# A value sweep of a graph network: two of eight tiles scaled by ScalarE and added by TensorE instead of VectorE

## The chip, the cores and the metric

The kernel runs on one core of a Trainium2 chip. The metric is the device time of one execution in microseconds. The engines are called by their names here: TensorE (PE in the profile, PEld for its weight loads), VectorE (DVE), ScalarE (ACT), GpSimd (POOL) and SyncE (SP, which issues DMA transfers). A q behind an engine's name is its sequencer.

## The reference, cut to what matters

The program is a stack of four graph layers on 3125 nodes and 50000 edges, sorted by their target. Layer 2 is a pair of attention layers; the second of them has two heads of 128 channels. Its last step is the one that the change touches:

```python
def transformer_conv(x, src, dst, Wq, bq, Wk, bk, Wv, bv, Ws, bs, H, C, concat):
    ...
    v = (x @ Wv + bv).reshape(n, H, C)
    ...
    out = jax.ops.segment_sum(p[:, :, None] * v[src], dst, num_segments=n)
    out = out / denom[:, :, None]
    out = out.reshape(n, H * C) if concat else out.mean(axis=1)
    return out + x @ Ws + bs
```

Here H = 2, C = 128 and concat is false: the two heads are averaged. For each edge the values of both heads are weighted by their softmax weights, added, and summed over the edges of each target node. All in float32.

## The kernel before, in words

**Tiles.** The sorted edges are laid out as 416 tiles of 128 edges (one per partition). Each tile belongs to one block of 128 target nodes; the block's number is data, and stands in a table. A loop over all tiles is called a sweep. It runs 13 times (G) over four groups of eight tiles (S4 = 4, HU = 8). A group is called a half in the code, and half m = 4i + h. So a sweep has 52 halves. The ring buffer has four slots, one for each h.

**The sweep L2F.** The softmax weights of both heads lie in `alpha` (already divided by the denominator and halved). SyncE loads 1 MB per half from DRAM into the ring slot (lines 676 to 680, `values_in`): eight tiles of 256 values per edge, head 0 first, head 1 behind. It does so once TensorE has counted `ring_free`. Four engines then work on a half:
- VectorE (`mix`, lines 1675 to 1687): copies the weights of the half into `relw` (L1680), waits for the loaded rows, scales head 1 of all eight tiles in one operation (L1682), waits for TensorE's product of the half before the last and makes the one-hot matrices of edge and target (L1684 by way of the helper on L1092), waits for ScalarE's eight scalings, and adds head 0 to head 1 (L1687).
- ScalarE (`scale_l2f`, lines 1926 to 1934): waits for the copied weights and for the rows, and scales head 0 of the eight tiles, one activation each, by a scalar per partition (L1934).
- TensorE (`sums_f`, lines 2394 to 2405): loads the eight block numbers into registers (helper on L461), waits for one-hots and addition, and multiplies one-hot by mixed values, one product per tile, into the PSUM columns of the tile's block (L2401). In the trace one such float32 product is two LDWEIGHTS and two MATMUL instructions. Behind the last product it waits until it is done and frees the ring slot (L2404, L2405).

The order is fixed by hand, through semaphores: each engine has its own program of 52 halves. `relw` and the one-hots have two buffers (s = h % 2). The key line of TensorE:

```python
for k in range(HU):
    last = M.matmul(psum_blocks[:, ds(blocks[k], 1), :], ohv[:, (h % 2) * HU + k, :],
                    ring256[:, h * HU + k, F:2 * F].unsqueeze(1), start=False, stop=False)
```

Ahead of the sweep stands the softmax of layer 2 (all engines wait for it), and behind it VectorE adds the sums of all blocks to the node values (L1691) and layer 3 begins.

Of the kernel before, what the change touches and what calls it, by code (L numbers as in the profile page):

```python
# [25 lines left out]
def gnn_stack(nc, a, out):  # L26
    f32, bf16, i32 = mybir.dt.float32, mybir.dt.bfloat16, mybir.dt.int32
    ALU, ACT, AX = mybir.AluOpType, mybir.ActivationFunctionType, mybir.AxisListType.X
    ds = bass.ds
    x_in, src_in, dst_in, w_in = a["x"], a["src"], a["dst"], a["edge_weight"]  # L30

    P, F = 128, 128
# [6 lines left out]
    HU = 8  # L39
# [5 lines left out]
    U = S4 * HU  # L45
# [19 lines left out]
    with ctx:  # L65
        def sb(name, shape, dt=f32):
            return ctx.enter_context(nc.sbuf_tensor(name, shape, dt))

        def sem(name):
            return ctx.enter_context(nc.semaphore(name))  # L70
# [27 lines left out]
        alpha = sb("alpha", [P, T, 4])  # L98
# [23 lines left out]
        def carve(at, shape, dt=f32):  # L122
            return view(work, at, shape, dt)
# [7 lines left out]
        ring256 = carve(0, [U, 256])  # L131
# [21 lines left out]
        ohv = carve(8192, [2 * HU, P])  # L153
# [7 lines left out]
        relw = sb("relw", [P, 2, HU, 5])  # L161
# [103 lines left out]
        psum_blocks = psf[:, 0:NP].rearrange("p (b f) -> p b f", f=P)  # L265
# [106 lines left out]
        def ph(name):  # L372
            if name not in made:
                made[name] = sem(name)
            return made[name]
# [25 lines left out]
        VALUES = [2 * SENT[g] * HU * 16 + CB * 16 for g in range(NS)]  # L401
        assert NS == CH
        HEADS = (4, 4, 2)

        def softmax_order(H):
            late = [step for h in range(H) for step in ([("merged", h)] + ([("inverse", h - 1)] if h else []))]
            return [("shifted", h) for h in range(H)] + late + [("inverse", H - 1)]

        def sm_step(n, what, h):
            return sum(len(softmax_order(H)) for H in HEADS[:n]) + softmax_order(HEADS[n]).index((what, h)) + 1  # L410

        def sm_made(n, what, h):
            return 2 * sum(HEADS[:n]) + (HEADS[n] if what == "safe" else 0) + h + 1

# [6 lines left out]
        def half_no(i, h):  # L421
            return i * S4 + h
# [27 lines left out]
        def values_reloaded(i, h):  # L450
            return values_copied(G - 1, h) + (i + 1) * 16
# [13 lines left out]
        def tiles_of(i, h):  # L465
            return ds(i * U + h * HU, HU)
# [433 lines left out]
        def _(dve):  # L900
            V = nc.vector
# [189 lines left out]
            def one_hots(out_t, o, i, h, iota=iota_f[:, :]):  # L1091
                return V.tensor_tensor(out_t, rec[o][:, tiles_of(i, h), 1:2].to_broadcast([P, HU, P]),  # L1092
                                       iota.unsqueeze(1).to_broadcast([P, HU, P]), ALU.is_equal)
# [35 lines left out]
            with dve.Fori(0, CH) as i:  # L1129
                s = Steps(dve, ph("node_dve"), i, NLN, DONE["n0"])  # L1130
# [544 lines left out]
            def mix(i, h):  # L1675

                s = h % 2
                m = half_no(i, h)
                v = ring256[:, h * HU:(h + 1) * HU, F:2 * F]
                V.tensor_copy(relw[:, s, :, 1:3], alpha[:, tiles_of(i, h), 0:2]).then_inc(ph("L2F_weights"), 1)  # L1680
                dve.wait_ge(s_rows[h], values_reloaded(i, h))
                V.tensor_tensor(v, v, alpha[:, tiles_of(i, h), 1:2].to_broadcast([P, HU, F]), ALU.mult).then_inc(ph("L2F_mixed"), 1)  # L1682
                dve.wait_ge(ph("L2F_product"), m + 1)
                one_hots(ohv[:, s * HU:(s + 1) * HU, :], 1, i, h).then_inc(ph("L2F_onehot"), 1)  # L1684
                dve.wait_ge(ph("L2F_mixed"), 2 * m + 1)
                dve.wait_ge(ph("L2F_scaled"), m * HU + HU)
                V.tensor_tensor(v, v, ring256[:, h * HU:(h + 1) * HU, 0:F], ALU.add).then_inc(ph("L2F_mixed"), 1)  # L1687

            each_half(dve, mix)
            dve.wait_ge(ph("closed"), CLOSED["L2F"])  # L1690
            link(V.tensor_tensor(x[:, :, :], x[:, :, :], psum_blocks, ALU.add))  # L1691
# [38 lines left out]
        def _(act):  # L1730
            A = nc.scalar
# [194 lines left out]
            def scale_l2f(i, h):  # L1926

                s = h % 2
                m = half_no(i, h)
                act.wait_ge(ph("L2F_weights"), m + 1)  # L1930
                act.wait_ge(s_rows[h], values_reloaded(i, h))
                for k in range(HU):
                    v = ring256[:, h * HU + k, 0:F]
                    A.activation(v, v, ACT.Copy, scale=relw[:, s, k, 1:2]).then_inc(ph("L2F_scaled"), 1)  # L1934

            each_half(act, scale_l2f)

            root("n3")
# [13 lines left out]
        def _(pe):  # L1952
            M = nc.tensor
# [107 lines left out]
            with pe.Fori(0, CH) as i:  # L2061
                pe.wait_ge(ph("node_dve"), DONE["n0"] + i * NLN + NLN)
                for b in range(CB):
                    last = M.transpose(psf[:, b * P:(b + 1) * P], hs[:, b, :], ident[:, :])
# [3 lines left out]
                for b in range(CB):  # L2068
                    last = M.matmul(psf[:, 1024 + b * P:1024 + (b + 1) * P], hT[:, b * P:(b + 1) * P], w01[:, :],
                                    start=True, stop=True)  # L2070
# [56 lines left out]
            for bank in BANKS:  # L2127
                pe.wait_ge(ph("node_normed"), NORMED["n1"] + bank[-1] + 1)
                for b in bank:
                    last = M.transpose(psum_blocks[:, b, :], h_all[:, b, :], ident[:, :])  # L2130
                last.then_inc(ph("node_turned"), 1)
            for n, bank in enumerate(BANKS):
                pe.wait_ge(ph("node_hT"), HT["n1"] + n + 1)
                for b in bank:
                    nodes = hT_all[:, b * P:(b + 1) * P]
                    M.matmul(ps[:, 7, b * 8:(b + 1) * 8], nodes, watt[:, :], start=True, stop=True)
                    last = M.matmul(psum_blocks[:, b, :], nodes, wlin[:, :], start=True, stop=True)
# [91 lines left out]
            def blocks_of(o, i, h):  # L2229
                return loaded_blocks(mybir.EngineType.PE, o, i, h)  # L2230
# [95 lines left out]
            def by_heads(n, to, weights, last_head=0):  # L2326
                for h in range(4):
                    if last_head and h > 1:
                        pe.wait_ge(ph("n2b_h1"), last_head + h - 3)
                    last = M.matmul(to, acc[:, n, h * P:(h + 1) * P], weights(h), start=h == 0, stop=h == 3)  # L2330
                return last
# [22 lines left out]
            for n in range(NB):  # L2354
                if n >= 2:
                    pe.wait_ge(ph("n2b_evac"), NB + 2 + max(n - 3, -1))
                last = by_heads(n, ps[:, 4 + n % 4, 0:256], lambda h: wq2[h // 2][:, h % 2, :])
                if n < OVERWRITTEN:
                    last = by_heads(n, ps[:, 4 + n % 4, 256:384], lambda h: ws2[:, h, :])
# [35 lines left out]
            def sums_f(i, h):  # L2395
                m = half_no(i, h)
                blocks = blocks_of(1, i, h)
                pe.wait_ge(ph("L2F_onehot"), m + 1)
                pe.wait_ge(ph("L2F_mixed"), 2 * m + 2)
                for k in range(HU):  # L2400
                    last = M.matmul(psum_blocks[:, ds(blocks[k], 1), :], ohv[:, (h % 2) * HU + k, :],  # L2401
                                    ring256[:, h * HU + k, F:2 * F].unsqueeze(1), start=False, stop=False)
                last.then_inc(ph("L2F_product"), 1)
                pe.wait_ge(ph("L2F_product"), m + 3)  # L2404
                pe.sem_inc(ph("ring_free"), 1)  # L2405

            each_half(pe, sums_f)
            close_sums(7, zero_f).then_inc(ph("closed"), 1)

# [54 lines left out]
```

## Time and profile before

| | us |
|---|---|
| median of three runs | 5294.79 |
| lowest and highest | 5293.7, 5297.85 |
| span of the profiled execution, first to last instruction | 5289.8 |
| TensorE, VectorE, ScalarE, GpSimd busy in the span | 2873.2, 2794.9, 791.8, 3461.7 |
| sweep L2F, first weight copy to last product | 4482.15 to 4691.09 |

The profile is of one execution. No time of its own is given for it apart from its span; the median of the runs is 5.0 us above that span, which holds what lies ahead of the first and behind the last instruction. Busy time of TensorE counts overlapping matmuls once, and "idle before" is the time in which the engine ran nothing just ahead of the instruction. The name behind it is inferred: it is whoever last fulfilled a semaphore that the instruction waited for, even if that was long before. "Issue" means that nothing such was found. Granted clock 1.0 is 2.4 GHz, 0.5 is 1.2 GHz.

### The profile page before, as it was taken

The page shows a single profiled execution, that of the slowest core. Times are in us where ns is not written, and L with a number is a line of the kernel's source. Part 1 is how long each engine was busy: PE and PEld are TensorE (multiplying, and loading weights), DVE is VectorE, ACT ScalarE, POOL GpSimd, SP SyncE. Part 2 cuts the span into 40 slices and gives each one's busy share as a digit, 9 for nine tenths or more (in the row PEclk, how much of TensorE's full clock was granted, in tenths as well). Part 3 has the DMA queues.
Part 4 walks back from the last instruction along what each step waited for, and adds up shares of the span by engine and source line. Part 5 has one row for each costly group of instructions (what it writes and reads, how often), then busy time and mean ns, then how long its engine had stood idle before and what let it go on. Part 6 is the DMA issues. An engine that isn't in the chain of part 4 may idle for free.

```text
span 5289.8 us, 73813 instructions
## 1 busy us (share of the span) xinstructions
PE 2873.2 (54%) x17389; PEld 2236.2 (42%) x17390; DVE 2794.9 (53%) x6391; ACT 791.8 (15%) x3180; POOL 3461.7 (65%) x3922
## 2 busy tenths in 40 slices
PE   5443477763333573034445877768986665643333
PEld 5333366653333463034443333356464333543333
DVE  8889822223221588033335988876147666971111
ACT  2121100000000100000001555456100001640000
POOL 3777677767777777777774777654047773017775
PEclk9999955555555555556556999878997766876566
DMA  2211222231112483033333444534169997732223
GB/s 62 67 29 47 68 52 52 52 46 26 27 27 25 60 115 47 18 69 79 81 81 59 137 127 127 133 91 139 40 191 316 335 331 221 268 124 52 52 52 53
DMA packets 303759, 526.16 MB, mean 99 GB/s; under 512 B 89450, under 2 KB 172640, under 8 KB 296928
## 3 DMA queue, kind: packets, MB, share of 16 engines
q1 hardware_dynamic: 177960, 289.53, 19.3%
q0 software_dynamic: 125728, 235.82, 18.3%
q8 instruction: 27, 0.44, 0.0%
q14 instruction: 44, 0.36, 0.0%
HBM read 423.29 MB, written 101.80 MB: 99 GB/s over the span
## 4 chain that ended last, share of the span: by engine, by line
POOL 42%; issue 28%; DVE 14%; PE 9%; DMA 2%; ACT 2%; DVEq 2%; POOLq 1%; SPq 1%; ACTq 0%; PEldq 0%
POOL work L789 31%; POOL rec_by_dst L749 6%; PE ps L2330 3%; POOL acc L789 2%; DVE acc L1568 2%; ACT work L1934 1%; DVE work L1027 1%; PE ps L2104 1%; POOL idx_slot L783 1%; PE ps L2045 1%; DVE work L1015 1%; PE ps L2401 1%; DVE work L973 1%; DVE work L1042 1%; DVE acc L1496 1%
## 5 line engine op out<-in xcount | busy, mean ns | idle before, releaser
L789 POOL DMA_INDIRECT work<-t_h,idx_slot x832 | 801.2, 963 | 546.2 <-DMA t_h<-acc 304.5
L2045 PE MATMUL ps<-work 128*128 128x128 f32 (+1 forms) x2496 | 700.0, 443 | 677.2 <-DMA work<-t_v,idx_slot 352.0
L789 POOL DMA_INDIRECT work<-t_v,idx_slot x832 | 789.2, 949 | 267.0 <-issue 221.9
L2045 PEld LDWEIGHTS ps<-work 128*128 128x128 f32 x2496 | 583.2, 328 | 700.5 <-issue 700.5
L789 POOL DMA_INDIRECT work<-t_xl,idx_slot x416 | 413.5, 994 | 123.8 <-issue 111.0
L2298 PE MATMUL ps<-big,work 128*128 x832 | 411.3, 647 | 105.7 <-DVE work L1246 68.9
L749 POOL DMA_INDIRECT rec_by_dst<-sc_rec_d,sc_idx x392 | 394.1, 1005 | 113.2 <-issue 104.6
L749 POOL DMA_INDIRECT rec_by_src<-sc_rec_s,sc_idx x392 | 388.6, 991 | 113.3 <-issue 104.2
L2370 PE MATMUL ps<-big,work 128*128 x832 | 326.4, 549 | 191.7 <-DVE aS L1630 153.5
L1102 DVE COPY relw<-rec_s 128x16 f32 x104 | 19.7, 189 | 672.8 <-PE ps L2045 672.2
L789 POOL DMA_INDIRECT work<-t_kv,idx_slot x208 | 201.3, 968 | 257.7 <-DMA t_kv<-big 173.1
L2370 PEld LDWEIGHTS ps<-big,work 128*128 128x128 f32 x832 | 206.0, 268 | 311.6 <-issue 280.1
L2250 PE MATMUL ps<-work 128*128 128x128 f32 x832 | 196.0, 430 | 206.4 <-DVE work L1445 206.4
L1496 DVE TENSOR_TENSOR acc<-ps,work 128x512 f32<-128x512 f32 x416 | 278.9, 681 | 49.6 <-PE ps L2298 26.8
L2298 PEld LDWEIGHTS ps<-big,work 128*128 128x128 f32 x832 | 161.7, 204 | 317.1 <-issue 317.1
L2044 PEld LDWEIGHTS ps<-one_column,work 128*128 128x128 f32 x832 | 222.9, 327 | 167.7 <-issue 167.7
L1876 ACT ACTIVATE acc<-acc 128x128 f32<-128x128 f32 x832 | 250.0, 301 | 247.7 <-DVE acc L1496 247.2
L1092 DVE TENSOR_TENSOR work<-rec_d,ps 128x1024 f32<-128x1024 f32 x52 | 63.1, 1220 | 409.3 <-PE ps L2045 408.7
L1105 DVE TENSOR_SCALAR work<-ps,relw 128x128 f32<-128x128 f32 x832 | 274.5, 401 | 3.8
L2250 PEld LDWEIGHTS ps<-work 128*128 128x128 f32 x832 | 181.4, 330 | 211.0 <-issue 211.0
L2044 PE MATMUL ps<-one_column,work 128*128 128x1 f32 x832 | 183.7, 290 | 152.4 <-DMA work<-t_v,idx_slot 145.6
L789 POOL DMA_INDIRECT acc<-t_kv,idx_slot x208 | 202.7, 975 | 66.1 <-issue 54.9
(480 smaller groups left out, 6177.0 us busy)
## 6 DMA issues: line engine op xcount, KB each, us to landing
work<-rows_of_v_by_position SPq DMA_DIRECT2D x52, 1024.0 KB
work<-relT_by_dst SPq DMA_DIRECT2D x156, 256.0 KB
rows_of_h_by_position<-work SPq DMA_DIRECT2D x52, 512.0 KB
work<-rows_of_h_by_position SPq DMA_DIRECT2D x52, 512.0 KB
rows_of_v_by_position<-work SPq DMA_DIRECT2D x26, 1024.0 KB
rows_of_v_by_position<-acc SPq DMA_DIRECT2D x26, 1024.0 KB
work<-t_v,idx_slot POOLq DMA_INDIRECT x832
work<-relT_by_src SPq DMA_DIRECT2D x52, 256.0 KB
```

Of the source, the lines that this page charges most:

```text
L749: nc.gpsimd.indirect_dma_start(rec_dram[o], bass.IndirectOffsetOnAxis(ap=sc_idx[:, h * HU + k:h * HU + k + 1], axis=0), sc_rec[o][:, h * H ...
L789: nc.gpsimd.indirect_dma_start(to, None, table, bass.IndirectOffsetOnAxis(ap=idx_slot[:, h * HU + k:h * HU + k + 1], axis=0)).then_inc(s_g ...
L1105: last = V.tensor_scalar(oh[:, h * HU + k, :], iota_p, pair[:, k, 0:1], pair[:, k, 1:2], ALU.is_equal, ALU.mult)
L1496: V.tensor_tensor(prod[:, k, :].rearrange("p (h c) -> p h c", h=4), q, g, ALU.mult).then_inc(sig("L2A", "_multiplied"), 1)
L1568: V.tensor_tensor(part, part, ps[:, k, 0:4 * WN].rearrange("p (h j) -> p h j", j=WN), ALU.add).then_inc(ph("L2C_added"), 1)
L1876: ins = A.activation(q, q, ACT.Copy, accum_out=aS[:, s * HU + k, hd:hd + 1])
L2044: M.matmul(weights_sum[:, ds(b, 1)], oh[:, s, :], one_column[:, :], start=False, stop=False)
L2045: ins = M.matmul(psum_blocks[:, ds(b, 1), 0:width], oh[:, s, :], ring[:, h * HU + k, 0:width].unsqueeze(1), start=False, stop=False)
L2250: last = M.matmul(psum_blocks[:, ds(blocks[k], 1), :], oh[:, (h % 2) * HU + k, :], ring140[:, h * HU + k, 0:F].unsqueeze(1), start=False, ...
L2298: M.matmul(q_bank(h, k).unsqueeze(1), ohT[:, s, k * P:(k + 1) * P], big[:, ds(blocks[k], 1), :], start=True, stop=True).then_inc(sig("L2A" ...
L2330: last = M.matmul(to, acc[:, n, h * P:(h + 1) * P], weights(h), start=h == 0, stop=h == 3)
L2370: last = M.matmul(ps[:, k % 4, 0:256].unsqueeze(1), ohT[:, s, k * P:(k + 1) * P], q2[:, ds(blocks[k], 1), :], start=True, stop=True)
```

## The change

Of each half's eight tiles, six (MIXED) are treated as before. For the other two, VectorE neither scales nor adds; ScalarE scales both heads (SCALED = 2 x 8 - 6 = 10 activations per half instead of 8), and TensorE sums each head with a product of its own, with the same one-hot matrix, into the same PSUM columns. TensorE waits for all ten scalings ahead of the seventh tile. VectorE waits for the first six scalings of a half only. Its wait for TensorE's product of the half before the last moves from ahead of the one-hots to ahead of the weight copy.

```diff
--- before.py
+++ after.py
@@ -401,6 +401,8 @@
         VALUES = [2 * SENT[g] * HU * 16 + CB * 16 for g in range(NS)]
         assert NS == CH
         HEADS = (4, 4, 2)
+        MIXED = HU - 2
+        SCALED = 2 * HU - MIXED
 
         def softmax_order(H):
             late = [step for h in range(H) for step in ([("merged", h)] + ([("inverse", h - 1)] if h else []))]
@@ -1676,15 +1678,15 @@
 
                 s = h % 2
                 m = half_no(i, h)
-                v = ring256[:, h * HU:(h + 1) * HU, F:2 * F]
+                v = ring256[:, h * HU:h * HU + MIXED, F:2 * F]
+                dve.wait_ge(ph("L2F_product"), m + 1)
                 V.tensor_copy(relw[:, s, :, 1:3], alpha[:, tiles_of(i, h), 0:2]).then_inc(ph("L2F_weights"), 1)
                 dve.wait_ge(s_rows[h], values_reloaded(i, h))
-                V.tensor_tensor(v, v, alpha[:, tiles_of(i, h), 1:2].to_broadcast([P, HU, F]), ALU.mult).then_inc(ph("L2F_mixed"), 1)
-                dve.wait_ge(ph("L2F_product"), m + 1)
+                V.tensor_tensor(v, v, alpha[:, ds(i * U + h * HU, MIXED), 1:2].to_broadcast([P, MIXED, F]), ALU.mult).then_inc(ph("L2F_mixed"), 1)
                 one_hots(ohv[:, s * HU:(s + 1) * HU, :], 1, i, h).then_inc(ph("L2F_onehot"), 1)
                 dve.wait_ge(ph("L2F_mixed"), 2 * m + 1)
-                dve.wait_ge(ph("L2F_scaled"), m * HU + HU)
-                V.tensor_tensor(v, v, ring256[:, h * HU:(h + 1) * HU, 0:F], ALU.add).then_inc(ph("L2F_mixed"), 1)
+                dve.wait_ge(ph("L2F_scaled"), m * SCALED + MIXED)
+                V.tensor_tensor(v, v, ring256[:, h * HU:h * HU + MIXED, 0:F], ALU.add).then_inc(ph("L2F_mixed"), 1)
 
             each_half(dve, mix)
             dve.wait_ge(ph("closed"), CLOSED["L2F"])
@@ -1930,8 +1932,9 @@
                 act.wait_ge(ph("L2F_weights"), m + 1)
                 act.wait_ge(s_rows[h], values_reloaded(i, h))
                 for k in range(HU):
-                    v = ring256[:, h * HU + k, 0:F]
-                    A.activation(v, v, ACT.Copy, scale=relw[:, s, k, 1:2]).then_inc(ph("L2F_scaled"), 1)
+                    for head in range(1 if k < MIXED else 2):
+                        v = ring256[:, h * HU + k, head * F:(head + 1) * F]
+                        A.activation(v, v, ACT.Copy, scale=relw[:, s, k, 1 + head:2 + head]).then_inc(ph("L2F_scaled"), 1)
 
             each_half(act, scale_l2f)
 
@@ -2398,8 +2401,11 @@
                 pe.wait_ge(ph("L2F_onehot"), m + 1)
                 pe.wait_ge(ph("L2F_mixed"), 2 * m + 2)
                 for k in range(HU):
-                    last = M.matmul(psum_blocks[:, ds(blocks[k], 1), :], ohv[:, (h % 2) * HU + k, :],
-                                    ring256[:, h * HU + k, F:2 * F].unsqueeze(1), start=False, stop=False)
+                    if k == MIXED:
+                        pe.wait_ge(ph("L2F_scaled"), (m + 1) * SCALED)
+                    for head in ((1,) if k < MIXED else (0, 1)):
+                        last = M.matmul(psum_blocks[:, ds(blocks[k], 1), :], ohv[:, (h % 2) * HU + k, :],
+                                        ring256[:, h * HU + k, head * F:(head + 1) * F].unsqueeze(1), start=False, stop=False)
                 last.then_inc(ph("L2F_product"), 1)
                 pe.wait_ge(ph("L2F_product"), m + 3)
                 pe.sem_inc(ph("ring_free"), 1)
```

## Rows read from the trace of the kernel before

**Rows 1.** The page: its first line, and the chain of work by engine.

```profile
span 5289.8 us, 73813 instructions
...
POOL 42%; issue 28%; DVE 14%; PE 9%; DMA 2%; ACT 2%; DVEq 2%; POOLq 1%; SPq 1%; ACTq 0%; PEldq 0%
```

**Rows 2.** Windows: stretch, length; busy PE, PEld, DVE, ACT, POOL; granted clock, DMA share, GB/s.

```profile
4486.00:4691.00 205.00, 125.82 (x832) 115.27 (x832) 182.55 (x205) 126.02 (x409) 0.00 (x0) 0.86 0.72 246
...
3060.00:3140.00 80.00, 65.30 (x195) 27.87 (x194) 71.78 (x163) 44.13 (x259) 62.22 (x71) 0.94 0.44 130
...
3520.00:3670.00 150.00, 129.80 (x726) 107.31 (x725) 105.27 (x368) 117.19 (x467) 87.92 (x46) 0.99 0.53 154
```

**Rows 3.** Groups by line, 4482 to 4692 us: busy us, mean ns, idle before, releasers.

```profile
L1934 ACT ACTIVATE work<-work,relw 128x128 f32<-128x128 f32 x416 | 127.2, 388 | 75.3 <-DVE relw L1680 75.3
...
L2401 PE MATMUL ps<-work 128*128 128x128 f32 x832 | 125.9, 314 | 80.3 <-DVE work L1682 34.2 <-DVE work L1092 25.8 <-issue 15.6
...
L1687 DVE TENSOR_TENSOR work<-work 128x1024 f32<-128x1024 f32 x52 | 63.6, 1224 | 13.2 <-ACT work L1934 13.1
...
L1092 DVE TENSOR_TENSOR work<-rec_d,iota_f 128x1024 f32<-128x1024 f32 x52 | 63.4, 1218 | 5.1 <-PE ps L2401 5.1
...
L1682 DVE TENSOR_TENSOR work<-work,alpha 128x1024 f32<-128x1024 f32 x52 | 63.3, 1218 | 0.1
```

**Rows 4.** Timeline of VectorE and ScalarE (start us, us): first addition, then one round.

```profile
4484.93 1.23 DVE L1687 TENSOR_TENSOR work<-work 128x1024 f32<-128x1024 f32 x1 [0.19 <-ACT work L1934]
...
4560.46 1.22 DVE L1682 TENSOR_TENSOR work<-work,alpha 128x1024 f32<-128x1024 f32 x1
...
4563.16 1.22 DVE L1687 TENSOR_TENSOR work<-work 128x1024 f32<-128x1024 f32 x1 [0.34 <-ACT work L1934]
...
4564.30 0.17 DVE L1680 COPY relw<-alpha 128x16 f32 x1
...
4564.50 2.44 ACT L1934 ACTIVATE work<-work,relw 128x128 f32<-128x128 f32 x8 [1.38 <-DVE relw L1680]
```

**Rows 5.** Timeline of TensorE's halves in the sweep: start us, us, instructions, idle before.

```profile
4486.31 3.78 PE L2401 MATMUL ps<-work 128*128 128x128 f32 x16 [1.45 <-DVE work L1687]
...
4491.66 2.05 PE L2401 MATMUL ps<-work 128*128 128x128 f32 x16 [1.58 <-DVE work L1682]
...
4546.16 2.05 PE L2401 MATMUL ps<-work 128*128 128x128 f32 x16 [1.39 <-DVE work L1682]
...
4550.11 2.58 PE L2401 MATMUL ps<-work 128*128 128x128 f32 x16 [1.91 <-DVE work L1682]
...
4554.17 3.78 PE L2401 MATMUL ps<-work 128*128 128x128 f32 x16 [1.48 <-DVE work L1682]
...
4559.34 2.05 PE L2401 MATMUL ps<-work 128*128 128x128 f32 x16 [1.39 <-DVE work L1092]
...
4562.80 2.05 PE L2401 MATMUL ps<-work 128*128 128x128 f32 x16 [1.41 <-issue]
...
4689.04 2.05 PE L2401 MATMUL ps<-work 128*128 128x128 f32 x16 [1.41 <-issue]
```

**Rows 6.** Line 461 in the sweep, TensorE's sequencer: durations in ns, min/median/max.

```profile
L461 PEldq TENSOR_LOAD <-block_of_tile_d x104: 327/331/334, 4482.2 to 4688.4; - x104
...
L461 PEldq FUSED_REGOPS  x91: 46/46/46, 4482.6 to 4688.3; - x91
```

**Rows 7.** Waits of SyncE's queue in the sweep (us, times, longest), and one load, issue to landing.

```profile
SPq L678 <- PEq L2405: 189.2, 48, 41.0
...
4627.12 4.65 DMA work<-rows_of_v_by_position
```

**Rows 8.** Groups by line and shape: a 640-wide VectorE operation elsewhere.

```profile
L1702 DVE TENSOR_TENSOR acc<-acc,rows 128x640 f32<-128x640 f32 x5 | 4.1, 824 | 0.2
```

**Rows 9.** Timelines cut short: seven instructions at full clock, six at low clock.

```profile
4562.80 1.04 PE L2401 MATMUL ps<-work 128*128 128x128 f32 x7 [1.41 <-issue]
...
4554.17 1.64 PE L2401 MATMUL ps<-work 128*128 128x128 f32 x6 [1.48 <-DVE work L1682]
```


## The prediction

> **What bounds the kernel now.** I read the page first, for the span and the chain [rows 1]. The chain names GpSimd for 42% of the whole kernel, which says nothing about the stretch that the diff touches. So I looked for that stretch: the value sweep of layer 2 runs from the first weight copy at 4482.15 us to the last product at 4691.09 us, 4% of the span. GpSimd does nothing in it [rows 2].
>
> Inside it the share of busy time points at VectorE: 182.55 of 205 us, 89%, against 61% for TensorE and 61% for ScalarE [rows 2]. Per half of eight tiles VectorE runs a copy, the scaling of head 1, the one-hots and the addition, each large one about 1.22 us [rows 3], and comes round every 3.8 to 3.9 us: in [rows 4] the scaling of head 1 begins 3.84 us before the next copy. Before its addition it waits 0.34 us for ScalarE's eight scalings (2.44 us). ScalarE in turn waits for the weights, which VectorE copies only after the addition. That is a loop of two engines at 3.87 us.
>
> TensorE has to be read in another way, by its order in time [rows 5]. A half is 16 matmul instructions (two for each of eight products) and takes 2.05 us at 2.4 GHz or 3.78 us at 1.2 GHz. Between two halves stand 1.4 to 1.5 us, or 1.9 us once in four halves, where the loop turns (one early gap has 1.58). These gaps name a VectorE line or "issue" as what ended them, but their length does not change with it: 1.39 us stands with either of two VectorE lines, 1.41 us with "issue". In the gap the sequencer waits for its own last product, frees the ring slot and loads the next eight block numbers (two loads of 0.331 us [rows 6] and register work). So the named releaser had long been done, and the gap is TensorE's own. The account closes: 52 halves are busy for 125.9 us, the gaps are 80.3 us less the 1.45 us ahead of the first, and 125.9 + 78.9 = 204.8 us [rows 3]; from first to last product the trace has 4689.04 + 2.05 - 4486.31 = 204.8 us [rows 5]. **TensorE is never kept waiting in the sweep**. At its mean clock it needs 3.94 us per half, slightly more than VectorE's 3.87, and VectorE is sometimes held back by it: 5.1 us ahead of the one-hots [rows 3]. Of the 125.9 us, 52 x 2.05 = 106.6 would be left at full clock; 19.3 us are the price of the low clock (mean 0.86 in [rows 2]).
>
> The transfers are not the limit: SyncE spends 189.2 us waiting for TensorE's free slots, and a load lands 4.65 us after issue [rows 7], while its slot is wanted three halves later.
>
> **The change part by part.**
> - VectorE: scaling and addition shrink from 1024 to 768 elements. A 640-wide one takes 0.824 us [rows 8] and a 1024-wide one 1.22, so 768 takes about 0.96: 0.53 us less per half. Cover: none of it is on TensorE's path, so I count it at nothing. VectorE would go to about 3.3 us per half, then wait for TensorE.
> - ScalarE: ten scalings instead of eight, 2.44 / 8 x 2 = 0.61 us more, 3.05 us per half. VectorE waits for the first six only (1.83 us). TensorE waits for all ten, in the middle of its half. This is hidden as long as ScalarE needs less than TensorE's period of 4.0 us.
> - TensorE: two products more per half, four instructions. Their spacing at full clock is (2.05 - 1.04) / (16 - 7) = 0.112 us and at low clock (3.78 - 1.64) / (16 - 6) = 0.214 us [rows 5, 9]. At full clock 52 x 4 x 0.112 = **+23.3 us**. The gaps stay.
> - The new wait of TensorE before tile six has no row like it. Lower bound nothing, because the sequencer runs ahead of the array; a gain is excluded, since nothing is taken away. Upper bound: a stop of one semaphore step, about 0.05 us as in [rows 6]'s register work, 2.6 us in all. I take nothing, since [rows 5] show 16 instructions without a break although each tile has its own address step. Behind it are queued only the two last tiles' products, and then the freeing of the slot.
> - The moved wait: VectorE now waits for the product of two halves before ahead of the weights, not ahead of the one-hots. Queued behind it are copy, scaling, one-hots and addition, and ScalarE waits for the copy. From that product on, about 0.1 + 0.96 + 1.22 + 0.96 = 3.2 us pass to the end of the addition (3.3 us to the end of ScalarE's tenth). TensorE needs the half only after gap, half and gap, 1.4 + 2.5 + 1.4 = 5.3 us. Cost nothing, with 2 us of cover. No DMA queue is passed: SyncE waits only for freed slots, and they come later, so the loads have more time.
> - The low clock. Lower bound: nothing, all halves at 2.4 GHz. Upper bound: the same share as now, 19.3 x 129.9 / 106.6 = 24 us. Each fall follows a long gap and shows in two halves, as in [rows 5], (2.58 - 2.05) + 1.73 = 2.3 us; the sweep has eight such pairs besides the low first half. A low half would now be busy 4.6 of 6.1 us, 75%, near the dense stretches with 82% and 87% busy, where the granted clock is 0.94 and 0.99 [rows 2]; a half at full clock is busy 2.5 of 4.0, 62%, near the sweep as it is. So I expect it to fall as often but to come back in half the time: 12 us, **7 us less** than the 19.3 of now.
> - The start: the first addition waits 0.19 us [rows 4]; with that and two shorter steps (0.27 each) TensorE begins 0.7 us earlier. **-0.7 us**. The end is TensorE's last product, as before.
>
> Sum: 23.3 - 7.3 - 0.7 = +15.3 us on a span of 5289.8, that is 5305.1. The median of the three runs, 5294.79, stands 5.0 us above that span (start and end of the execution), so the forecast is **5310 us**.
>
> The Trainium skill, Perfetto Trace Analysis, section Identifying the Most-Contended Engine, says to find the engine with the highest occupancy and to optimize that one first. By it VectorE with 89% would be the bound and the change a gain; the order in time disagrees.
>
> **Rivals.**
> - VectorE is the bound (the other side). Place: the additions at the end of VectorE's round. Price: 52 x 0.53 = 27.6 us gained, 5267 us. For it: 89% busy, and 60.0 of TensorE's 80.3 idle us name a VectorE line [rows 3]. Against it: the constant gaps. It decides from the point where TensorE's half plus gap is shorter than VectorE's round; with twenty instructions it is 2.50 + 1.55 = 4.05 us at best, above today's 3.87. Chance 0.05.
> - The clock stays up: twenty instructions per half keep TensorE at 2.4 GHz throughout. 52 x 2.50 + 78.9 = 208.8 us of sweep, +3.3 with the earlier start, 5298 us. For it: 0.99 in the densest stretch. Against it: the long gap of 1.91 us, ahead of each fall, is still there. Chance 0.10. The Trainium skill, TensorE: Matmul & The Clock Gate, Part 1, states that the gate is closed by default and activity opens it; more activity would then mean the full clock. The trace agrees in direction only: the denser stretches have the higher clock.
> - The moved wait closes a circle: product, weights, ten scalings, product. If its 3.3 us were 2.5 us longer than I think (a scaling slowed by transfers, say), TensorE would wait 0.5 us per half: 26 us more, 5336 us. Against it: ScalarE's groups last 2.44 or 2.45 us under the same transfers. Chance 0.04.
> - The change doesn't do what it says: the output or the order is the same as before and the time 5295. The counts in the diff (ten scalings, six awaited) fit each other. Chance 0.01.
> - My forecast, TensorE bound with a partly lower clock: 0.80.
>
> **How the numbers follow.** The forecast alone has a low-clock term between 0 and 24 us, 5298 to 5322, and with the bound of the mid-half wait and a few us between runs up to 5326. That with the full-clock case is the range, 5298 to 5326. About 0.2% (10.6 us) is what a measurement of this kernel can tell from no change. The full-clock case and the lower part of the forecast (a low-clock term under 7 us) lie within it, 0.10 + 0.08, and the case of no change 0.01: 0.19. Faster is the first rival, 0.05. The rest is slower, 0.76.
>
> **What would show it.** Right: L2401 with 1040 matmuls, busy for 140 to 145 us, the gaps unchanged at 1.4 and 1.9 us, the sweep at 221 us from first to last product; VectorE's waits move to the product (about 0.7 us per half, ahead of the weights); ScalarE's groups of 3.05 us. Wrong: gaps of TensorE that grow and vary, a wait on L1934 ahead of a product, or a sweep under 205 us. The clock term is wrong if the granted clock in the sweep stays at 0.86 or reaches 1.

## The result, and the profile after

The changed kernel takes 5310.26 us (median of six runs, 5308.27 to 5318.01) against 5294.24 us of the kernel before (six runs): ratio 1.0032, 95% interval 1.0022 to 1.0042. That is **16 us slower**. The forecast was 5310 us. The profiled execution took 5315.45 us with a span of 5313.0. The stretch of interest, from first to last product of the sweep, has 4710.76 + 2.49 - 4491.66 = 221.6 us; before it had 204.8. These 16.8 us account for the whole difference of the medians, 16.0 us. The span grew by 23.2 us: 5.35 us of it lie ahead of the changed lines (the first product comes that much later than before), and 1.0 us behind the sweep. In experiments 1 to 4 the first product came between 4484.64 and 4489.16 us, so this start scatters by some us.

First the window of the sweep after, columns as in [rows 2]:

```profile
4491.00:4713.00 222.00, 142.19 (x1040) 133.08 (x1040) 159.93 (x205) 156.54 (x514) 0.00 (x0) 0.93 0.66 227
```

VectorE went from 182.55 to 159.93 us of busy time, and the time rose all the same. TensorE went from 125.82 to 142.19 us, and its granted clock from 0.86 to 0.93. The same stretch by line, to be held against [rows 3]:

```profile
L1937 ACT ACTIVATE work<-work,relw 128x128 f32<-128x128 f32 x520 | 157.7, 388 | 63.3 <-DVE relw L1683 63.3
L2407 PE MATMUL ps<-work 128*128 128x128 f32 x1040 | 142.5, 298 | 79.9 <-DVE work L1685 77.8 <-issue 1.4 <-DVE work L1689 0.7
...
L1094 DVE TENSOR_TENSOR work<-rec_d,iota_f 128x1024 f32<-128x1024 f32 x52 | 63.3, 1218 | 0.0
L1685 DVE TENSOR_TENSOR work<-work,alpha 128x768 f32<-128x768 f32 x52 | 49.8, 958 | 1.7
L1689 DVE TENSOR_TENSOR work<-work 128x768 f32<-128x768 f32 x52 | 49.4, 951 | 0.0
L1683 DVE COPY relw<-alpha 128x16 f32 x52 | 9.2, 177 | 59.2 <-PE ps L2407 56.1 <-PEq L2395 3.0
```

TensorE's account again: 142.5 us busy and 79.9 us idle, of which 0.75 stand ahead of the first half; 142.5 + 79.15 = 221.6. The idle time is what it was before (78.9 us between halves). What is new is 56.1 us that VectorE waits for TensorE's product ahead of the weight copy (L1683), and ScalarE's waits behind it. TensorE in order of time, the answer to [rows 5]:

```profile
4491.66 4.61 PE L2407 MATMUL ps<-work 128*128 128x128 f32 x20 [0.75 <-DVE work L1689]
4497.74 2.49 PE L2407 MATMUL ps<-work 128*128 128x128 f32 x20 [1.48 <-DVE work L1685]
4501.65 2.49 PE L2407 MATMUL ps<-work 128*128 128x128 f32 x20 [1.42 <-DVE work L1685]
...
4521.68 2.49 PE L2407 MATMUL ps<-work 128*128 128x128 f32 x20 [1.38 <-DVE work L1685]
4526.08 3.96 PE L2407 MATMUL ps<-work 128*128 128x128 f32 x20 [1.91 <-DVE work L1685]
4531.52 2.49 PE L2407 MATMUL ps<-work 128*128 128x128 f32 x20 [1.47 <-DVE work L1685]
4535.42 2.49 PE L2407 MATMUL ps<-work 128*128 128x128 f32 x20 [1.42 <-DVE work L1685]
...
4710.76 2.49 PE L2407 MATMUL ps<-work 128*128 128x128 f32 x20 [1.39 <-issue]
```

And VectorE's first weight copy, from its timeline:

```profile
4488.30 0.18 DVE L1683 COPY relw<-alpha 128x16 f32 x1 [3.02 <-PEq L2395]
```

TensorE's gaps are 1.38 to 1.48 us, and 1.90 to 2.08 at the turn of the loop (before: 1.91 to 1.97), though VectorE now finishes each half longer ahead. The plainest sign is the time from the end of the addition that a half needs to the start of that half. One pair from the kernel before (its addition is the one at 4563.16 in [rows 4], which ends at 4564.38), then one from the changed kernel:

```profile
4566.78 1.97 PE L2401 MATMUL ps<-work 128*128 128x128 f32 x16 [1.94 <-DVE work L1092]
...
4566.46 0.95 DVE L1689 TENSOR_TENSOR work<-work 128x768 f32<-128x768 f32 x1
4569.44 2.49 PE L2407 MATMUL ps<-work 128*128 128x128 f32 x20 [1.42 <-DVE work L1685]
```

That is 2.40 us of slack before and 2.03 us after. Over all halves but the first the slack is 0.81 to 3.80 us before and 2.01 to 4.30 us after. Only the first half of the sweep starts 0.15 us behind its addition, and so waits for it. (The addition is the last thing that a half needs from VectorE; the one-hots end before it.) Nearly all gaps of the changed kernel name the same line, L1685, the scaling of head 1, which is not what TensorE waits for; the name tells nothing here, and the slack does. A half is 2.49 us at full clock. The low clock shows in one half at a time (3.96 us at 4526.08), where in [rows 5] it showed in two.

### The profile page after: what moved, and what is told of

It is laid out like the page before. It is cut to its first block, busy times and chain, and to the rows that moved or that the text cites. A ratio compares the mean times of both kernels' runs of the same rounds, so it can differ in the third digit from the quotient of the medians.

```text
span 5313.0 us, 74385 instructions
## 1 busy us (share of the span) xinstructions
PE 2885.2 (54%) x17597; PEld 2250.0 (42%) x17598; DVE 2769.1 (52%) x6391; ACT 822.3 (15%) x3284; POOL 3462.3 (65%) x3922
## 3 DMA queue, kind: packets, MB, share of 16 engines
q1 hardware_dynamic: 177960, 289.53, 19.4%
## 4 chain that ended last, share of the span: by engine, by line
POOL 41%; issue 27%; DVE 15%; PE 11%; DMA 2%; DVEq 2%; POOLq 1%; SPq 1%; ACT 1%; ACTq 0%; PEldq 0%
POOL work L791 31%; POOL rec_by_dst L751 6%; PE ps L2333 3%; PE ps L2407 3%; POOL acc L791 2%; DVE acc L1570 2%; DVE work L1029 1%; PE ps L2107 1%; POOL idx_slot L785 1%; PE ps L2048 1%; DVE work L1685 1%; DVE work L1017 1%; DVE work L975 1%; DMA work<-t_v,idx_slot 1%; DVE work L1044 1%
```

## The experiments

Theory T: TensorE bounds the sweep, with its products and a gap of its own sequencer. Its rivals: VectorE's round bounds it (V), or the moved wait closes a circle (C). All experiments change only the sweep. The sweep is measured from first to last product in the profiled execution. The total time is the median beside the kernel before of the same group.

**1. VectorE's relief alone.** The kernel before, `mix` over six tiles:

```diff
-v = ring256[:, h * HU:(h + 1) * HU, F:2 * F]
+v = ring256[:, h * HU:h * HU + 6, F:2 * F]
...
-V.tensor_tensor(v, v, ring256[:, h * HU:(h + 1) * HU, 0:F], ALU.add)...
+V.tensor_tensor(v, v, ring256[:, h * HU:h * HU + 6, 0:F], ALU.add)...
```

The weights in the scaling of head 1 are cut to the same six tiles.

> The kernel before, with VectorE scaling and adding only six of the eight tiles of each half; ScalarE (eight scalings) and TensorE (sixteen instructions) are untouched. Left out: head 0 and the weight of head 1 in two of eight tiles. If TensorE bounds the sweep: from first to last product 204 to 205 us as before, gaps of 1.4 and 1.9 us as before, the time within 3 us of the kernel before; VectorE only waits longer for the product. If VectorE's round bounds it: 52 x 0.53 = 28 us less, a sweep of 177 us, 5267 us.

Measured: 5294.18 us against 5295.1, ratio 0.9999 (0.9989 to 1.0009); sweep 203.0 us. The groups by line of its sweep:

```profile
L2401 PE MATMUL ps<-work 128*128 128x128 f32 x832 | 124.2, 311 | 80.0 <-DVE work L1092 65.0 <-DVE work L1682 12.4 <-issue 1.4
...
L1092 DVE TENSOR_TENSOR work<-rec_d,iota_f 128x1024 f32<-128x1024 f32 x52 | 63.7, 1224 | 32.0 <-PE ps L2401 31.8
L1687 DVE TENSOR_TENSOR work<-work 128x768 f32<-128x768 f32 x52 | 49.7, 956 | 9.7 <-ACT work L1934 8.9
```

Some 27 us of VectorE's work left and nothing came of it: its waiting for TensorE ahead of the one-hots grew from 5.1 to 31.8 us. V falls. (The sweep is 1.8 us shorter than before. TensorE is busy for 1.7 us less at the same number of instructions, and a half at full clock is 2.05 us in both: the low clock took 17.6 us here and 19.3 there.)

**2. The added products taken out of the changed kernel.**

```diff
-for head in ((1,) if k < MIXED else (0, 1)):
+for head in (1,):
```

> The changed kernel without the two extra products of a half: VectorE and ScalarE as changed, TensorE with sixteen instructions again, its wait for ten scalings kept. Left out: head 0 of two of eight tiles. If TensorE's four instructions are the whole cost: sweep back at about 204 us (52 x 2.05 + 78.9 + a low-clock term near 19), total near 5294. If the moved wait or the two more scalings cost anything: it stays over 5300 and the gaps of TensorE grow and vary.

Measured: 5295.5 us, ratio 1.0003 (0.9994 to 1.0013); sweep 206.1 us.

```profile
L1937 ACT ACTIVATE work<-work,relw 128x128 f32<-128x128 f32 x520 | 157.6, 388 | 48.8 <-DVE relw L1683 48.7
L2407 PE MATMUL ps<-work 128*128 128x128 f32 x832 | 127.0, 316 | 79.9 <-DVE work L1685 77.7 <-issue 1.4 <-DVE work L1689 0.7
...
L1683 DVE COPY relw<-alpha 128x16 f32 x52 | 9.2, 178 | 44.5 <-PE ps L2407 41.5 <-PEq L2395 3.0
```

The moved wait, the ten scalings and TensorE's wait amid the half are all still there, and the loss is gone. So these three cost nothing that the time or the gaps show. The sweep is 1.3 us longer than before, again by TensorE's low clock (20.4 us of it).

**3. The added products alone, in the kernel before.**

```diff
 for k in range(HU):
-    last = M.matmul(..., ring256[:, h * HU + k, F:2 * F].unsqueeze(1), ...)
+    for head in ((1,) if k < 6 else (0, 1)):
+        last = M.matmul(..., ring256[:, h * HU + k, head * F:(head + 1) * F].unsqueeze(1), ...)
```

> The kernel before, with a second product (head 0 region) for two of eight tiles and nothing else changed: VectorE and ScalarE do all of their old work. Changed in the result: head 0 of those two tiles is counted twice. If TensorE bounds the sweep: 52 x 2.49 + 78.9 + 12 = 220 us or so, total 5310, the same as the changed kernel, because VectorE's round of 3.87 us stays under 4.05. If VectorE's round bounds it: no more than 3 us above the kernel before.

Measured: 5308.23 us, ratio 1.0028 (1.0017 to 1.0038); sweep 220.6 us.

```profile
L2402 PE MATMUL ps<-work 128*128 128x128 f32 x1040 | 141.8, 297 | 80.3 <-DVE work L1092 77.4 <-DVE work L1687 1.4 <-issue 1.4
...
L1092 DVE TENSOR_TENSOR work<-rec_d,iota_f 128x1024 f32<-128x1024 f32 x52 | 63.7, 1225 | 31.8 <-PE ps L2402 31.5
```

Four instructions more per half reproduce the loss, with all of VectorE's work in place. TensorE's busy time, 141.8 us, is that of the changed kernel within 1 us. With 2 and 3 the cause is shown from both sides.

**4. The wait put back.** The changed kernel, with VectorE's wait ahead of the one-hots again:

```diff
-dve.wait_ge(ph("L2F_product"), m + 1)
 V.tensor_copy(relw[:, s, :, 1:3], alpha[:, tiles_of(i, h), 0:2])...
 ...
+dve.wait_ge(ph("L2F_product"), m + 1)
 one_hots(ohv[:, s * HU:(s + 1) * HU, :], 1, i, h)...
```

> The changed kernel with VectorE's wait for the product put back to where it was, ahead of the one-hots. If the moved wait is covered by TensorE's own work (my account: 2 us of cover): same sweep of 221 us, same 5310. If it closes a circle of product, weights and scalings: several us less than the changed kernel, with TensorE's gaps shorter.

Measured: 5311.14 us, ratio 1.0032 (1.0021 to 1.0044), the changed kernel's own; sweep 221.1 us.

```profile
L2407 PE MATMUL ps<-work 128*128 128x128 f32 x1040 | 142.1, 297 | 79.7 <-DVE work L1094 72.2 <-issue 6.9 <-DVE work L1689 0.6
...
L1094 DVE TENSOR_TENSOR work<-rec_d,iota_f 128x1024 f32<-128x1024 f32 x52 | 63.7, 1225 | 60.8 <-PE ps L2407 60.8
```

VectorE's wait moved back to the one-hots and has about the same size (60.8 us). C falls for the changed kernel: where VectorE waits for TensorE makes no difference while it has to wait anyway.

**5 to 8. TensorE's own gap.** If the gap is the loading of the next block numbers and not a wait, then loading them while the products run must shorten it. The products are all issued by then; the sequencer does the loads ahead of its wait for their end. In the first half behind the turn of the loop they stay where they were:

```diff
-def sums_f(i, h):
+def sums_f(i, h, blocks):
     m = half_no(i, h)
-    blocks = blocks_of(1, i, h)
     ...
     last.then_inc(ph("L2F_product"), 1)
+    nxt = blocks_of(1, i, h + 1) if h < S4 - 1 else None
     pe.wait_ge(ph("L2F_product"), m + 3)
     pe.sem_inc(ph("ring_free"), 1)
+    return nxt
...
-each_half(pe, sums_f)
+with pe.Fori(0, G) as i:
+    blocks = blocks_of(1, i, 0)
+    for h in range(S4):
+        blocks = sums_f(i, h, blocks)
```

This group of four, and the two groups behind it, ran on other chips, on which the kernel before took 6702 to 6760 us. The 1400 us more lie outside the sweep, nearly all ahead of it: in the first trace of this group the first product of the sweep comes at 5850.30 us instead of 4486.31, and the first sort loop (L1971) alone ends at 818 us instead of 413. The kernel before was not traced there, so its sweep is taken as the 204.8 us of the first chip; the changed kernel, traced on both, has 221.6 and 221.8 us. So in this part differences in microseconds say more than ratios. Totals scatter more than sweeps: in the four traces of this group the first product comes between 5813.71 and 5850.30 us, while what follows the last one lasts 663.7 to 665.5 us.

Early loading in the kernel before (5):

> The kernel before, with TensorE's block numbers of the next half loaded while the products of this half still run (for three of four halves; the first after the turn of the loop is as before). If the gap is TensorE's own sequencer work, three of four gaps shrink from 1.4 to 0.3 or 0.5 us where nothing else is late, and then the round of VectorE and ScalarE (3.87 us per half) bounds the sweep: about 201 us instead of 205, total 5288 to 5293, with waits of TensorE on VectorE's addition that vary. If the gap is a wait for VectorE or for the product, it stays and the time too.

Measured: 6693.99 against 6702.02 us, ratio 0.9988 (0.9966 to 1.001), by itself no change that can be told; sweep 199.3 us. Its timeline:

```profile
5901.03 2.05 PE L2400 MATMUL ps<-work 128*128 128x128 f32 x16 [0.49 <-PE ps L2400]
...
5903.10 1.22 DVE L1687 TENSOR_TENSOR work<-work 128x1024 f32<-128x1024 f32 x1 [0.33 <-ACT work L1934]
...
5904.46 2.05 PE L2400 MATMUL ps<-work 128*128 128x128 f32 x16 [1.39 <-DVE work L1687]
...
5906.93 1.23 DVE L1687 TENSOR_TENSOR work<-work 128x1024 f32<-128x1024 f32 x1 [0.26 <-ACT work L1934]
...
5908.29 1.86 PEld L2400 LDWEIGHTS ps<-work 128*128 128x128 f32 x16 [1.97 <-issue]
...
5910.84 1.22 DVE L1687 TENSOR_TENSOR work<-work 128x1024 f32<-128x1024 f32 x1 [0.34 <-ACT work L1934]
```

Now the gap varies, from 0.40 to 1.86 us apart from the turn of the loop, and the releaser is mostly the addition (L1687). It is a real wait this time: an addition ends at 5903.10 + 1.22 = 5904.32 and the half begins at 5904.46, the next ends at 5908.16 and the half begins at 5908.29. A start 0.13 to 0.15 us behind its addition is what a real wait looks like in these traces. VectorE and ScalarE bound the sweep, at 3.8 to 3.9 us per half.

Early loading in the changed kernel (6):

> The changed kernel with the same early loading of block numbers. If TensorE's own gap is what turned the change into a loss: TensorE needs 2.49 + (1.9 + 3 x 0.35) / 4 = 3.23 us per half at full clock, VectorE and ScalarE need about 3.2, a 1 MB load about 3.4 to 3.5. The sweep falls from 221 to 175 to 190 us, the total to 5268 to 5282, below the kernel before. If the gap is a wait for others: no difference.

Measured: 6662.08 us, 39.9 under the kernel before, ratio 0.9946 (0.992 to 0.9973); sweep 177.6 us.

```profile
L2406 PE MATMUL ps<-work 128*128 128x128 f32 x1040 | 134.7, 287 | 43.7 <-DVE work L1685 23.6 <-DVE work L1689 13.8 <-PE ps L2406 6.3
...
L1683 DVE COPY relw<-alpha 128x16 f32 x52 | 9.0, 172 | 22.4 <-PE ps L2406 19.4 <-PEq L2395 3.0
```

```profile
5899.45 2.49 PE L2406 MATMUL ps<-work 128*128 128x128 f32 x20 [0.48 <-DVE work L1689]
5904.02 2.40 PE L2406 MATMUL ps<-work 128*128 128x128 f32 x20 [2.07 <-DVE work L1685]
5906.91 2.49 PE L2406 MATMUL ps<-work 128*128 128x128 f32 x20 [0.49 <-PE ps L2406]
5909.92 2.49 PE L2406 MATMUL ps<-work 128*128 128x128 f32 x20 [0.52 <-DVE work L1689]
5912.90 2.49 PE L2406 MATMUL ps<-work 128*128 128x128 f32 x20 [0.49 <-DVE work L1689]
```

The first of these two blocks has the groups by line, the second TensorE's halves. Three of four gaps are 0.48 to 0.52 us now, the one at the turn of the loop is as it was (1.90 to 2.08 us), and the idle time fell from 79.9 to 43.7 us. VectorE's waits for the product fell from 56.1 to 19.4 us. The total gained more than the expected 5268 to 5282 us would mean (13 to 27 us under a kernel before of 5295); the sweep gives 27 of the 39.9 us.

These gaps are as even as those of the changed kernel, and yet two of them in every four halves are waits:

```profile
5908.83 0.95 DVE L1689 TENSOR_TENSOR work<-work 128x768 f32<-128x768 f32 x1
5911.80 0.96 DVE L1689 TENSOR_TENSOR work<-work 128x768 f32<-128x768 f32 x1
```

The additions end at 5909.78 and 5912.76 us, and the halves start 0.14 us behind each, at 5909.92 and 5912.90. So it goes in the third and fourth half of every turn, while the first two have 1.47 us of slack or more (but for the very first half of the sweep). The waits are short, since TensorE's shortest gap with early loads is 0.40 us (in experiment 5), but TensorE and VectorE are now about even. In the third half even C's chain closes: the product that ends at 5906.42 releases the weight copy at 5906.58, and VectorE works without a break from there to 5909.78. What putting the moved wait back would give here was not run. The transfers are not the limit: SyncE still waits 164.1 us for free slots, and the DMA engines are busy for 0.80 of the time. The 3.4 to 3.5 us that this expectation and that of experiment 8 give for a load are shown by no run; 283 GB/s at that busy share would make it about 3 us, as an estimate.

More products per half, with the gap left as it is (7; MIXED = HU - 4, four tiles each way):

> The changed kernel with four of eight tiles mixed by VectorE and four added by TensorE (twelve scalings, 24 matmul instructions per half). TensorE bound: 52 x (2.49 + 0.45) + 78.9 + a low-clock term of about 13 = 245 us, total 5333, i.e. as much above the changed kernel as it is above the one before, and somewhat more. VectorE bound: below the changed kernel.

Measured: 6738.2 us, 36.2 above the kernel before, ratio 1.0048 (1.003 to 1.0066); sweep 242.1 us.

```profile
L2407 PE MATMUL ps<-work 128*128 128x128 f32 x1248 | 163.2, 291 | 79.1 <-DVE work L1685 71.3 <-issue 7.6 <-DVE work L1689 0.2
```

TensorE has 163.2 us of work and still 79.1 of gaps. From eight to six to four mixed tiles the sweep goes 204.8, 221.6, 242.1 us: 16.8 and 20.5 us more for 208 instructions more each time, while VectorE has less to do each time (the expectation of 245 us was 3 us too high).

Early loading with seven mixed tiles (8):

> Early loading of block numbers, with seven of eight tiles mixed by VectorE (nine scalings, 18 matmul instructions). Per half VectorE about 3.4 us, ScalarE 2.7, TensorE 2.27 + 0.74 = 3.0, a load 3.4 to 3.5. Within 5 us of the same kernel with six mixed tiles, and below both kernels: 5268 to 5285.

Measured: 6678.59 us, 23.4 under the kernel before, ratio 0.9963 (0.994 to 0.9985); sweep 181.2 us.

```profile
L2406 PE MATMUL ps<-work 128*128 128x128 f32 x936 | 122.4, 287 | 59.9 <-DVE work L1689 58.5 <-PE ps L2406 1.5
...
L1689 DVE TENSOR_TENSOR work<-work 128x896 f32<-128x896 f32 x52 | 56.8, 1092 | 5.5 <-ACT work L1937 2.3
```

TensorE's 59.9 us of gaps now name the addition for 58.5, and the starts bear it out:

```profile
5907.23 1.09 DVE L1689 TENSOR_TENSOR work<-work 128x896 f32<-128x896 f32 x1
5908.47 2.27 PE L2406 MATMUL ps<-work 128*128 128x128 f32 x18 [1.13 <-DVE work L1689]
```

This half starts 0.15 us behind the end of its addition (5908.32), with a gap of 1.13 us. With seven mixed tiles VectorE's round bounds the sweep again; it waits only 2.3 us for ScalarE and 3.0 us for TensorE in all. The two kernels are 3.6 us apart in the sweep, within the 5 expected; their totals are 16 us apart, more than the sweep explains, and both scatter by 30 us and more on this chip. Where the rest comes from stays open.

**The version that beats both, again.** Its expectations and those of its companions:

> The changed kernel with early loading of block numbers, a second time, since the group of runs before it ran with a kernel before of 6702 us, 1400 us of it outside this sweep. If the gain lies in the sweep alone, it is the same number of microseconds wherever the rest stands: a sweep of 178 us, 27 us less than the 205 of the kernel before, and a total 24 to 32 us under the kernel before beside it (5263 to 5270 where that is 5294).

> The kernel before with early loading of block numbers, a second time: a sweep of 199 to 201 us, bounded by the round of VectorE and ScalarE (52 x 3.87 = 201), 4 to 6 us under the kernel before beside it, with TensorE's gaps of changing length (0.5 to 2 us) and its starts at the ends of VectorE's additions.

> The changed kernel with early loading of block numbers, a third time, beside the changed kernel itself in the same group. A sweep of 178 us; 24 to 32 us under the kernel before and 40 to 48 us under the changed kernel, on whichever chip.

> The changed kernel as it is: a sweep of 221 to 222 us and 15 to 17 us above the kernel before of the same group, on whichever chip, because the difference is TensorE's work in the sweep.

| kernel | sweep, us | less the kernel before of its group, us | ratio and interval |
|---|---|---|---|
| changed, early loads, 2nd | 175.7 | -47.4 | 0.9936 (0.9912 to 0.9961) |
| before, early loads, 2nd | 201.1 | -25.9 | 0.9976 (0.9958 to 0.9995) |
| changed, early loads, 3rd | 177.6 | -27.8 | 0.9958 (0.9938 to 0.9978) |
| changed, again | 221.8 | +16.1 | 1.0018 (0.9995 to 1.0042) |

The interval of the changed kernel includes no change here; it also holds the 1.0032 of the first measurement. The sweeps repeat within 2 us on every chip. The total times scatter much more on these chips: in three groups the changed kernel with early loads is 39.9, 47.4 and 27.8 us under the kernel before, where its sweep is 27 to 29 us shorter than 204.8. For the last two 24 to 32 us were expected, and only the third measurement is there. The second run of the kernel before with early loads gained 25.9 us where its sweep gives 4 and 4 to 6 were expected. These misses have no cause in the sweep, and they stay open. Side by side on one chip, the changed kernel with early loads is 43.9 us under the changed kernel (6732.59 and 6776.46), and the sweeps differ by 44.2. On a chip of the first kind it was not run; by the sweep alone it would stand near 5294 - 27 = 5267 us there, as an estimate.

## Why the prediction was right

Point by point, by its own steps:

- **TensorE never waits in the sweep**: shown, but for the first half. Relieving VectorE alone changed nothing (1), the gaps kept their length in the changed kernel and in experiments 1 to 4 and 7, whose VectorE and ScalarE had different loads, and every half but the first starts 0.8 us or more behind its addition. One step of the argument proved nothing: "the account closes" holds for any engine, since busy and idle time always add up to the stretch.
- **Four instructions per half, +23.3 us at full clock**: a half has 2.49 us instead of 2.05, 52 x 0.44 = 22.9 us. The gaps added 0.25 us (79.15 instead of 78.9).
- **The low clock, 12 us where 19.3 were**: measured is 142.5 - 52 x 2.49 = 13.0. The granted clock of the sweep rose to 0.93. Two more kernels with twenty instructions and long gaps have 12.3 (3) and 12.6 us (4), so the size repeats. The reason I gave, as many falls and each half as dear, holds only roughly: behind the first half, seven halves lose 1.5 us each, where eight pairs lost 2.2. That is one fall fewer, each at two thirds of the price and not at half. The two misses cancel, and the number was the middle of a range of 24 us: that it met so well is partly luck.
- **Start, -0.7 us**: from the first weight copy to the first product it was 4486.31 - 4482.15 = 4.16 us and is now 4491.66 - 4488.30 = 3.36, that is 0.8 less.
- **The wait amid the half and the moved wait, nothing**: shown by 2, 3 and 4. Twenty instructions run through in 2.49 us, less than the 2.50 of sixteen plus four spacings.
- **VectorE and ScalarE**: operations of 958 and 951 ns for the forecast 0.96 us, groups of 3.03 us for 3.05. VectorE's wait was given as 0.7 us per half; it is 56.1 / 52 = 1.1. I had set its round of 3.3 us against TensorE's 4.05 at full clock; the true numbers are about 3.2 and 4.26.
- **The sum**: from the first weight copy to the last product +15.3 us were forecast, and 224.95 - 208.94 = 16.0 are measured; the medians differ by 16.0 too. From first to last product it is 16.0 forecast against 16.8.
- **The 5.0 us between span and median** are not "start and end of the execution", as the prediction and the section on the time before have it. In every run a time stands 1.7 to 3.0 us above its own span; the rest of the 5.0 is that the profiled execution was shorter than the median one. As an offset from one execution to the median it did no harm.

The rule of the Trainium skill, Perfetto Trace Analysis, section Identifying the Most-Contended Engine (highest occupancy first), would have picked VectorE with its 89%. For TensorE that section goes by the busy time of the weight loads, here 115.27 of 205 us or 56%, which is lower still. Runs 1 and 3 show that TensorE, with 61% in its matmuls, was the bound. Its other 39% were gaps in which no other engine held it up, and experiment 6 took almost half of that idle time away by moving the loads of the block numbers. The same page's section Optimization Strategy asks which semaphore a gap waits for, and that question leads right: here the only semaphore that TensorE waits for inside the gap is the one that its own last product counts.

The rival that the clock stays up failed: the granted clock came to 0.93. All seven falls behind the first half begin in the half right behind the turn of the loop, as did the eight of before. But that long gap alone does not decide: with early loads it is still there, and the clock fell behind only two, one and two of the twelve turns in its three traces (granted clock 0.97, 0.98, 0.96). What the clock follows was not tested apart.

## What to carry to other kernels

Gaps of the same length whatever name stands behind them are a hint that an engine does not wait for others; they are no proof, since the even gaps of experiment 6 were partly waits. The proof is in the starts: hold each start against the end of what it needs. Slack of 0.8 us and more at every start is no wait, and 0.14 us at every start is one. An engine with slack everywhere can be the bound at 61% busy. Giving it work to relieve a busier one costs the length of that work (22.9 us here, less 6.3 that the higher clock gave back). First take the sequencer's own work out of the gap: here the same change is a loss of 16 us with the loads in the gap, and a gain of 22 and 25 us in the sweep (199.3 to 177.6, and 201.1 to 175.7) without them.

## What the runs showed that I had not expected

- Of the 1.4 us gap 0.9 to 1.0 us vanish when the two loads of 0.331 us and their register steps run under the products; 0.4 to 0.5 us stay. I put them down to the wait for the last product and the counting of the slot, which no run separates.
- On three other chips the kernel before takes 6702 to 6760 us instead of 5295. The changed kernel's sweep takes the same time on one of them to within 0.2 us. Why the rest differs was not looked into.
